# Norms that take two chunks in one logarithm and one exponential: 512-column against 1024-column instructions on ScalarE

## The reference, cut to what matters

```
pre:   h = norm(x)              # mean over the 128 features taken off, divided by sqrt(variance + eps)
y = layer(h)
post:  x = x + norm(y)
```

## Time and profile before

| | us |
|---|---|
| median of three runs | 1216.22 |
| own time of the profiled execution | 1216.37 |
| its span, first to last instruction | 1214.5 |
| TensorE busy | 971.9 |
| VectorE busy | 887.9 |
| GpSimd busy | 668.7 |
| ScalarE busy | 655.1 |

### The profile page before, as it was taken

One profiled execution on the slowest core, in us unless ns is written; L12 is line 12 of the kernel. 1 busy time (PEld: TensorE's weight loads), 2 busy tenths in 40 slices (PEclk: granted clock), 3 DMA queues, 4 the chain that ended last, 5 costly groups with the idle time before them and its releaser, 6 DMA issues.

```text
span 1214.5 us, 11589 instructions
## 1 busy us (share of the span) xinstructions
PE 971.9 (80%) x3048; PEld 556.8 (46%) x3048; DVE 887.9 (73%) x1190; ACT 655.1 (54%) x1183; POOL 668.7 (55%) x464
## 2 busy tenths in 40 slices
PE   6769787488779973599999999876768777775896
PEld 3324342133236622488888888532323233333784
DVE  4975886999967459366666666588999998735564
ACT  5843758200064482355656555778666575362555
POOL 3030466599920042277777777503998898632672
PEclk9979899599999996799999999988899898998899
DMA  2000300000020000466676666200000000001661
GB/s 74 1 0 0 115 1 16 0 0 1 0 61 1 13 4 7 100 158 147 141 158 145 148 154 139 56 0 1 0 0 1 0 1 0 1 13 40 142 145 35
DMA packets 18645, 61.29 MB, mean 50 GB/s; under 512 B 2560, under 2 KB 12416, under 8 KB 12800
## 3 DMA queue, kind: packets, MB, share of 16 engines
q1 hardware_dynamic: 18608, 60.86, 21.4%
HBM read 59.15 MB, written 1.70 MB: 50 GB/s over the span
## 4 chain that ended last, share of the span: by engine, by line
PE 45%; DVE 28%; POOL 10%; issue 8%; ACT 6%; DMA 2%; SPq 0%; POOLq 0%; DVEq 0%; ACTq 0%
PE ps L386 44%; POOL g L1223 6%; DVE g L1251 4%; DVE g L1475 3%; ACT g L798 2%; ACT rstd L798 2%; DVE resid L1251 2%; DVE tmp L1251 2%; DVE parts L1406 2%; DVE parts L1251 2%; DVE y L1726 2%; DVE g L1682 1%; POOL sq L1115 1%; POOL rstd L1232 1%; DMA g<-coef_scratch 1%
## 5 line engine op out<-in xcount | busy, mean ns | idle before, releaser
L386 PE MATMUL ps<-parts 128*128 128x512 f32 x1800 | 443.1, 404 | 38.8 <-DVE g L1251 13.4
L386 PEld LDWEIGHTS ps<-parts 128*128 128x128 f32 x1800 | 340.9, 192 | 140.2 <-DVE parts L1251 17.6
L1158 POOL TENSOR_TENSOR parts<-g,parts 128x512 fp32r<-128x512 f32 x168 | 217.8, 1297 | 156.8 <-ACT parts L798 152.8
L798 ACT ACTIVATE g<-ps 128x512 f32<-128x512 f32 (+2 forms) x302 | 178.6, 596 | 204.7 <-PE ps L386 176.0
L1251 DVE TENSOR_TENSOR ps<-g,ps 128x512 f32<-128x512 f32 x168 | 116.9, 696 | 110.4 <-PE ps L386 88.5
L386 PE MATMUL ps<-g,arena 128*128 128x512 f32 (+1 forms) x328 | 160.6, 631 | 40.8 <-POOL g L1210 18.0
L1223 POOL TENSOR_TENSOR g<-g 128x1024 f32<-128x1024 f32 x64 | 148.9, 2356 | 50.6 <-DVE g L1251 50.6
L1115 POOL TENSOR_TENSOR sq<-resid 128x512 f32<-128x512 f32 x32 | 36.0, 1125 | 199.5 <-DVE resid L1251 184.8
L798 ACT ACTIVATE parts<-g 128x512 fp32r<-128x512 f32 (+2 forms) x252 | 126.3, 533 | 36.2 <-DVE g L1251 19.2
L1251 DVE TENSOR_TENSOR g<-ps,g 128x512 f32<-128x512 f32 (+1 forms) x164 | 115.5, 704 | 40.9 <-DMA g<-coef_scratch 17.3
L386 PEld LDWEIGHTS ps<-g,arena 128*128 128x128 f32 (+1 forms) x328 | 62.5, 198 | 135.4 <-issue 61.5
(11 more groups left out here) (176 smaller groups left out, 1155.5 us busy)
## 6 DMA issues: line engine op xcount, KB each, us to landing
g<-coef_scratch SPq DMA_DIRECT2D x80, 512.0 KB, 6.2
g<-in_moe_dram SPq DMA_DIRECT2D x42, 192.0 KB, 4.9
g<-in_rope_dram SPq DMA_DIRECT2D x1, 2048.0 KB, 8.7
arena<-in_weights_dram SPq DMA_DIRECT2D x1, 1348.5 KB, 6.0
arena<-in_weights_dram SPq DMA_DIRECT2D x1, 1028.5 KB, 5.7
g<-in_x_dram SPq DMA_DIRECT2D x4, 256.0 KB, 4.2
out_dram<-g SPq DMA_DIRECT2D x4, 256.0 KB, 2.5
arena<-in_weights_dram SPq DMA_DIRECT2D x1, 838.0 KB, 7.3
```

What stands on the lines that cost most here:

```text
L386: return nc.tensor.matmul(o, lhsT, rhs, start=start, stop=stop, **kw)
L798: return nc.scalar.activation(o, i, func, **kw)
L1158: pv.tensor_tensor(hid_lo[:, cols(c)], g[:, 6, (c % 2) * N:(c % 2 + 1) * N], hid_hi[:, cols(c)].bitcast(F32), ALU.subtract).then_inc(s["hl ...
```

## The change

`rstd_of` goes over the four chunks in two steps instead of four. Each step waits until both chunks' variances are there, takes one Ln over the two banks (1024 columns) and one Exp over 1024 columns of `rstd`, and then adds 2 to `rstd_ready`. Nothing else changes: the waits of VectorE on `rstd_ready`, chunk by chunk, stand as they were.

```diff
             def rstd_of(name, eps, bank=4):
                 k = NORM[name]
-                for c in range(CHUNKS):
-                    act.wait_ge(s["var_ready"], k * CHUNKS + c + 1)
-                    chain(f(rstd[:, cols(c)], ps[:, bank + c, :], ACT.Ln, bias=eps))
+                for c in range(0, CHUNKS, 2):
+                    act.wait_ge(s["var_ready"], k * CHUNKS + c + 2)
+                    both = rstd[:, c * N:(c + 2) * N]
+                    chain(f(both, ps[:, bank + c:bank + c + 2, :].rearrange("p b n -> p (b n)"), ACT.Ln, bias=eps))
                     chain.wait()
-                    f(rstd[:, cols(c)], rstd[:, cols(c)], ACT.Exp, scale=-0.5).then_inc(s["rstd_ready"], 1)
+                    f(both, both, ACT.Exp, scale=-0.5).then_inc(s["rstd_ready"], 2)
```

## The result

The changed kernel takes 1246.45 us (median of 4 runs, 1244.72 to 1247.02), the kernel before beside it 1217.01 us: ratio 1.0241, 95% interval 1.0223 to 1.0259, or 29.4 us more. The forecast was 1243.3 us, range 1235 to 1250. The profiled execution is the shortest of the four, with 1244.72 us; its span is 1242.9 us, and TensorE's mean granted clock fell from 0.928 to 0.912.

What follows compares the result with a forecast made beforehand. The norms, where the whole kernel stands in one line, were taken to bound it by first and last chunk. Terms: 11.2 + 4.9 + 2.2 + 1.72 + 1.72 + 2.75 + 0.35 = 24.9; 1216.4 + 24.9 + 2 = 1243.3 us, range 1235 to 1250.

Steps and rivals of the forecast that it cites:

- Length of a pair: On ScalarE: Ln over two banks 1.11 us, Exp over 1024 columns 1.06; 2.24 us from Ln to product.
- The first chunk: In each post norm: 0.86 us wait for the second variance plus 0.86 longer instructions, first product 1.72 us later.
- The pre norm: At a boundary: last `normed` 1.09 us later on top of the post norm's 1.72, 2.81 in all.
- layers 5 and 7: Boundaries ahead of these layers: ScalarE's queue comes first, so 1.72 + 0.7 = 2.45 us each, twice = 4.9.
- Start and `rms`: Start: last products of `ln1` 2.75 us later; `rms`: loss on the first pair nearly won back, 0.35 us.
- Layer 2: ScalarE's copy of k behind the last Exp comes 2.20 us later, and the scans that follow inherit it: 2.2 us.
- Layer 6: Small VectorE and ScalarE steps stand behind the last `normed`, ahead of its convolution, so the full 2.81 us counts.
- Clock: TensorE's longer pauses over seven boundaries: 0 to 7 us, taken as 2; rival with all 7, 1248.4 us, chance 0.12.
- ScalarE's saved 15 us: Rival: ScalarE's time is what counts, each of 38 pairs gives 0.4 us: 1201 us, chance 0.05.
- Absorbed: Rival: layers behind hide the pre norms' extra wait, only first-chunk delay counts: 17 us, 1233.5 us, chance 0.13.
- Two banks cost more: Rival: Ln over two banks takes 1.37 us, 5 us more over some 18 pairs: 1248 us, chance 0.04.
- The signs of being wrong: Layers behind starting at unchanged distance from their boundary's first variance, or stages between boundaries changing by over 1 us each.

Runs made afterwards that it cites:

- the kernel with the wait alone: Kernel before with single 512-column Ln and Exp, but no Ln before both variances of its pair: 1235.51 us, ratio 1.0147.
- the pre norms alone: Pairs only in the seven pre norms behind layer 0 (pre1 to pre7), singles elsewhere as in the kernel before: 1226.27 us, ratio 1.0077.
- two variants of this kernel: Kernel before with the last chunk's square of seven pre norms moved from GpSimd to ScalarE, 1216.27 us; with the third chunk's square moved too, 1216.1 us.
- the kernel that hands on the first half: Changed kernel with Ln over two banks kept, but two 512-column Exp, each with its own increment: 1236.55 us, ratio 1.0164.
- the kernel with fillers: Changed kernel with matmuls of constants in TensorE's pauses between post and pre variances of the seven boundaries: 1244.78 us, ratio 1.0234.

## Why the prediction was right, and which terms were off

The mechanism is the one forecast, and the terms for single places came out within 0.1 us where the layer behind does not enter. That the total is as near as 3 us is in part luck: layers 2 and 6 took more than forecast, layer 7 took less, and the 2 us for the clock stood in the wrong place.

- *Length of a pair*: 1.11 and 1.06 us, as forecast. The step from Ln's end to Exp was 0.09 us instead of 0.03: 0.06 us in each post norm.
- *The first chunk*: 1.77 instead of 1.72 us, eight times over (1.61 behind layer 0). That it is half wait and half length is shown by the kernel with the wait alone, 0.86.
- *The pre norm*: 1.13 instead of 1.09 us behind the first product, with VectorE idle twice and GpSimd's last square at 1.04 us as forecast. In the boundaries ahead of layers 5 and 7 it is about 2.1 us, of which ScalarE's queue behind hides most, as forecast for layer 5 (2.64 for 2.45); layer 7 took 1.36 for the same 2.45, and no run tells why.
- *Start and `rms`*: 2.66 for 2.75 at the start, with a spread of 1 us from one execution to the next; in `rms` itself 0.43 us where the clock was the same, for 0.35.
- *Layer 2*: this step failed. I had it begin 2.2 us late, behind ScalarE's copy of k. That copy is 2.3 us late, but the first scan stands behind the last `normed` in VectorE's queue, and the whole 2.9 us pass through: 2.91 + 0.68 = 3.6 us with `rms` in the second execution, for 2.55. The first execution adds 2.5 us at a lower clock in two of layer 2's stretches.
- *Layer 6*: 2.81 forecast; 3.1 for the boundary and 1.2 more inside the layer, the same twice. The 1.2 are about half ahead of the scans (50.4 for 49.7 us) and half in them (207.0 for 206.4); I have no run that tells why.
- *Clock*: 2 us for the seven boundaries. The place was wrong. With the clock held up there, 0.9 us came back, within what can't be told from nothing; what it cost was inside layer 2, as much as 2.5 us in one execution and nothing in another. The Trainium skill (TensorE: Matmul & The Clock Gate, HAM oscillation) describes how waits between bursts of matmuls bring the array back to half clock. The trace agrees as to the fall, in seven of seven boundaries. That the upper bound would be the likelier did not follow: 7 us were not there. The prediction also had a variance at the lower clock come 0.4 to 0.8 us later; it is up to 0.95 (Ln at D + 6.37 for 5.42).
- *The rivals*: ScalarE's saved 15 us bought nothing that a run shows: the kernel with the third and fourth chunk paired has ScalarE busy for 2.1 us less and is slower. "Absorbed" falls too, with 9.4 us for the pre norms alone. "Two banks cost more" falls with Ln at 1.11 us.
- *The signs of being wrong*: one of them came. The prediction was to be wrong if stages between boundaries changed by more than 1 us each. Layers 2 and 6 did, by 3.1 and 1.2 us more (layer 2 by 0.7 in the second pair of profiles), and layers 5 and 7 by 1.2 and 2.6 us less. For layer 5 the prediction's own argument of ScalarE's queue covers it; layers 2, 6 and 7 it had not foreseen at this size.

Sum by the table and these terms: 2.7 + 1.8 + 1.8 for start, `ln2` and the last norm, 22.4 for the seven boundaries, 0.9 for what the layers between gave and took: 29.6 us between the two profiles, counted from the first work of TensorE (its input came 1.2 us earlier in the second profile, hence 28.4 between the spans). Between the second profiles of the two kernels it is 26.7 us; the difference is mostly the 2.5 us in layer 2. The forecast's 24.9 and 2 of clock is near the latter. The three executions of the changed kernel that were not profiled were 1.3 to 2.3 us longer than the profiled one, and no trace shows where.

## What to carry to other kernels

In a pipeline of chunks over several engines a wider instruction saves its fixed part and delays the first chunk by a whole second one: by the wait for its input and by its own length. Look at who waits for the first piece and who sets the pace; where the stage is not the pace-setter, the saving (here 15 us) bought nothing, and the delay (here 1.77 us eight times, 1.13 to 2.2 seven times) is paid wherever the engines stand in one line, less what another engine's queue hides behind it (here ahead of layers 5 and 7). Gains or losses under 0.3% can be given back far behind the place of the change, in part because a stretch can meet TensorE's lower clock in one execution and not in the next: two variants of this kernel had shorter boundaries, a third had its clock held up between the variances, and all three took the same time.

## What the runs showed of the hardware

- An Exp of 512 columns starts 0.03 us behind the end of the Ln that it waits for, be that of 512 columns (76 times in the kernel before) or of 1024 (38 times in the kernel that hands on the first half); an Exp of 1024 columns starts 0.09 us behind it (38 times in the changed kernel).
- One Ln over two PSUM banks takes 1.11 us, two over one bank each 0.69 and 0.67.
- VectorE's `resid` takes 0.69 us alone and 1.03 while GpSimd squares, GpSimd's square 1.04 us alone and 1.42 beside `normed`; an engine that is made late can so run the next steps faster. It gave back 0.32 of 0.48 us in the kernel with the third and fourth chunk paired.
- Identical code in layer 6 took 277.9 us in two profiles of the kernel before and 279.1 in two of the changed one, up to 280.6 in others, with a granted clock of 0.84 to 0.90 ahead of its scans (0.84 in the two longest).
- The clock fell to the lower level inside boundaries whose longest pause of TensorE was 1.4 to 1.5 us (kernel before, behind layers 4 and 6), and did not behind layers 1, 2, 3 and 5, with the same pauses; behind pauses of 3.2 us it fell in all fourteen boundaries of two profiles of the changed kernel. What it cost there lay between nothing (six boundaries of the first of these profiles, against the kernel with fillers) and 0.6 us (the first boundary of the second), and 0.9 us in one boundary of the kernel with the wait alone (16.19 for 15.26 us).
